# Layer 0 attention of a gated two-layer block: keys and values made once, relu on ScalarE, another TensorE order, and wide magic sums in the last ffn

## The reference

```
# layer 0 attention, x normalised first: 16 heads of 16 channels, scale = 16 ** -0.5
q = x_norm @ Wq + bq;  k = ctx @ Wk + bk;  v = ctx @ Wv + bv
attn = softmax(clip(q @ k.T * scale, -10000, 10000), axis=-1)
x = x + tanh(g) * ((attn @ v) @ Wo + bo)
...
# layer 1 ffn, hidden of 1024 channels in 8-bit weights and 16-bit activations
h = gelu(x_q @ W_in_q + b_in)
h_q = clip(round(h * s), -32768, 32767) / s,  s = 32767 / max(abs(h))
x = x + tanh(g) * (h_q @ W_out_q + b_out)
```

## Time and profile before

| | us |
|---|---|
| median of 3 runs | 1312.31 |
| the profiled execution, its own time | 1310.7 |
| its span | 1308.6 |
| attention of layer 0, from its first load to the last output tile | 7.0 to 325.1 |
| last block of the ffn, from its first magic sum | 1234.2 to the end |
| TensorE busy | 1180.4 (90%) |
| VectorE busy | 977.9 (75%) |
| ScalarE busy | 812.1 (62%) |
| GpSimd busy | 540.7 (41%) |

### The profile page before, as it was taken

How to read it: one execution, slowest core, us unless ns; L and a number is a source line. 1 busy time by engine, 2 the same in 40 slices (tenths; PEclk the granted TensorE clock), 3 DMA queues, 4 the chain that set the end, 5 groups by cost and what they waited for, 6 DMA issues and landing times. The chain is left out here.

```text
span 1308.6 us, 26405 instructions
## 1 busy us (share of the span) xinstructions
PE 1180.4 (90%) x8487; PEld 895.5 (68%) x8533; DVE 977.9 (75%) x2135; ACT 812.1 (62%) x2405; POOL 540.7 (41%) x523
## 2 busy tenths in 40 slices
PE   4989999897786599999999999975999999959898
PEld 3879888886443377777777777753777777735465
DVE  4988989895763356666666667745999999869798
ACT  2454646453466356666666665535888888739897
POOL 3666757674313322222222222106888889600000
PEclk9999999999799699999999999997999999979899
DMA  3223323221976425333333333215424242100133
GB/s 120 66 73 97 97 72 99 72 85 37 281 226 198 129 55 153 116 114 118 115 116 115 116 116 101 78 46 149 139 74 143 74 143 74 62 8 1 33 105 122
DMA packets 124157, 135.30 MB, mean 103 GB/s; under 512 B 13837, under 2 KB 108739, under 8 KB 123907
## 3 DMA queue, kind: packets, MB, share of 16 engines
q1 hardware_dynamic: 116577, 114.81, 28.2%
q0 software_dynamic: 6816, 18.62, 5.2%
q10 hardware_dynamic: 642, 0.33, 0.1%
HBM read 84.43 MB, written 49.29 MB: 102 GB/s over the span
## 5 line engine op out<-in xcount | busy, mean ns | idle before, releaser
L1424 ACT ACTIVATE exp_h<-exp_ps_h,exp_b_now 128x256 f32<-128x256 f32 x312 | 128.7, 463 | 159.8 <-PE exp_ps_h L1364 156.5
L1338 POOL DMA_INDIRECT exp_xg<-xn,all_token_of x78 | 94.5, 1212 | 311.6 <-PE exp_ps_x L1351 291.9
L1364 PE MATMUL exp_ps_h<-exp_xhi,exp_w_now 128*128 128x256 bf16 x1248 | 214.8, 276 | 4.5 <-DVE exp_xlo L1455 4.5
L1809 ACT ACTIVATE a_z<-a_ps_sc,a_nmx 128x77 f32<-128x77 f32 x512 | 159.2, 367 | 36.0 <-DVE a_nmx L1911 36.0
L1364 PE MATMUL exp_ps_h<-exp_xlo,exp_w_now 128*128 128x256 bf16 x624 | 172.1, 276 | 0.0
L1531 DVE TENSOR_TENSOR exp_hlo<-exp_h,exp_hhi 128x512 bf16<-128x512 f32 x156 | 106.9, 692 | 79.5 <-ACT exp_hhi L1428 76.9
L1376 PE MATMUL exp_ps_y<-moe_w2s,exp_hhi 128*128 x585 | 139.2, 379 | 2.0
L1364 PEld LDWEIGHTS exp_ps_h<-exp_xhi,exp_w_now 128*128 128x128 bf16 x1248 | 123.5, 99 | 20.6 <-issue 5.1
L1809 ACT ACTIVATION_READ_ACCUMULATOR a_z<-a_ps_sc,a_nmx 128x1 f32 x512 | 127.8, 250 | 0.0
L1776 PE MATMUL a_ps_o<-a_v_now,a_phi 128*128 128x256 bf16 (+1 forms) x640 | 106.6, 273 | 2.3 <-DVE a_plo L1900 2.3
L1428 ACT ACTIVATE exp_hhi<-exp_h 128x512 bf16<-128x512 f32 x156 | 98.3, 630 | 4.9
(11 more groups left out here) (243 smaller groups left out, 2858.8 us busy)
## 6 DMA issues: line engine op xcount, KB each, us to landing
a_stage<-in_L_ffn_W_dram SPq DMA_DIRECT2D x64, 256.0 KB
y_slots<-exp_y SPq DMA_DIRECT2D x78, 128.0 KB
fold_k<-route_kst SPq DMA_DIRECT2D x16, 308.0 KB, 4.2
fold_v<-route_vst SPq DMA_DIRECT2D x16, 308.0 KB
exp_job_in<-fold_k SPq DMA_DIRECT2D x14, 352.0 KB
exp_job_in<-fold_v SPq DMA_DIRECT2D x14, 352.0 KB
a_x<-in_x_dram SPq DMA_DIRECT2D x32, 128.0 KB, 2.5
x<-a_xo SPq DMA_DIRECT2D x32, 128.0 KB, 1.7
```

What stands on the lines that cost most here:

```text
L1338: pool.indirect_dma_start(out=xg[:, v, u, :], out_offset=None, in_=xn_dram[:, :], in_offset=bass.IndirectOffsetOnAxis(ap=at.bitcast(U32), ...
L1364: mm = pe.matmul(ps_h[:, i, f % 2 * SLOT_T:(f % 2 + 1) * SLOT_T], w1_now[:, v, k, hl, f * P:(f + 1) * P], xx[:, k, :], start=(q == 0), sto ...
L1424: ins = act.activation(h[:, f, :], ps_h[:, i, f % 2 * SLOT_T:(f % 2 + 1) * SLOT_T], ACT.Gelu_apprx_tanh, bias=b1_now[:, v, f:f + 1])
L1809: ins = act.activation(z[:, u, h * KEYS:(h + 1) * KEYS], ps_sc[:, j, (h - SB[j][0]) * KEYS:(h - SB[j][0] + 1) * KEYS], ACT.Exp, bias=nmx[: ...
```

## The change

In `attention` the keys and values of all four batches are multiplied once, near the start: keys of batch 0 before the loop, values in slot 0 (two pairs of batches, 8 matmuls of 256 columns), the keys of batches 1 to 3 in slot 1. ScalarE copies them to `kT` and `v_rows`. The block diagonals now have two buffers each; GpSimd sets them to zero once (four memsets instead of masks), and SyncE puts the keys and values of each batch in their places by transfers inside SBUF: 8 for the keys (slot t = 6 of the batch before) and 25 for the values (slots t = 2 to 5 of the batch before, four heads in each; for batch 0 all 25 in slot 1). TensorE waits for `k_in` at t = 0 and for `v_in` at t = 2. The functions `block_keys`, `block_values` and `context` are gone.

`min(z, 0)` on VectorE becomes `relu(-z)` on ScalarE, followed there by exp with the sign turned. z has three buffers. On TensorE the output projection comes right behind the queries, and the transposes of the probabilities go behind the scores. ScalarE copies the queries before relu and exp; VectorE takes the sums of exp behind the maxima; GpSimd adds the bias and makes one low half before the products with the reciprocals. All slots are written out, without a loop. `wq` and `bq` are loaded by ScalarE's queue on a semaphore of their own.

In the last block of `ffn` the magic sums are wide: VectorE does blocks 0 and 1 in one instruction of 1024 columns, ScalarE blocks 2 to 4 and 5 to 7 in two of 1536 columns. The group loop is written out.

```diff
+            def place_keys(b):
+                sp.wait_ge(s["kT_done"], 1 if b == 0 else 2)
+                wait(sp, s["scores_done"], NSB * TPB * (b - 1))
+                for h in range(hpg):
+                    rows = slice(h * dh, (h + 1) * dh)
+                    sp.dma_start(kblk[rows, b % 2, :, h * KEYS:(h + 1) * KEYS], kT[rows, :, b, :]).then_inc(k_in[b % 2], 16)
+            def place_values(b, h0, h1):
+                sp.wait_ge(s["v_rows_done"], b // 2 + 1)
+                wait(sp, s["pv_done"], TPB * (b - 1))
+                for h, r0, r1 in spans:
+                    if h0 <= h < h1:
+                        i = blocks.index((r0 // P, h // hpg))
+                        sp.dma_start(vblk[r0 % P:r0 % P + r1 - r0, b % 2, i, h % hpg * dh:(h % hpg + 1) * dh],
+                                     v_rows[r0 - h * KEYS:r1 - h * KEYS, b, h * dh:(h + 1) * dh]).then_inc(v_in[b % 2], 16)
...
# SyncE, end of a slot
+                if T == 1:
+                    sp.wait_ge(s["zero_done"], 4)
+                    place_values(0, 0, HEADS)
+                if t == 6 and b + 1 < B:
+                    place_keys(b + 1)
+                if 2 <= t < 6 and b + 1 < B:
+                    place_values(b + 1, 4 * (t - 2), 4 * (t - 2) + 4)
...
# TensorE
-                if has(T - 2):
-                    pe.wait_ge(s["norm_done"], T - 1)
-                    if t == 2:
-                        pe.wait_ge(s["v_done"], NVG * (b + 1))
...
                 if has(T - 3):
                     pe.wait_ge(s["attn_done"], T - 2)
...
+                if has(T - 2):
+                    pe.wait_ge(s["norm_done"], T - 1)
+                    if T == 2:
+                        pe.wait_ge(s["kT_done"], 2)
...
...
+                if T == 0:
+                    pe.wait_ge(weights_in, 16 * N_WEIGHTS)
+                    values(0, 2)
+                    values(1, 1)
+                if T == 1:
+                    pe.wait_ge(s["v_rows_done"], 2)
+                    keys(1, B, 0)
...
# ScalarE, behind attnT and qT
+                if has(T - 1):
+                    zt = z[:, (T - 1) % NZ, :]
+                    act.wait_ge(s["z_done"], NSB * T)
+                    act.activation(zt, zt, ACT.Relu, scale=-1.0).then_inc(s["zc_done"], 1)
+                    act.wait_ge(s["zc_done"], T)
+                    act.activation(zt, zt, ACT.Exp, scale=-scale).then_inc(s["exp_done"], 1)
...
# VectorE
-                    dve.wait_ge(s["z_done"], NSB * (T + 1))
-                    dve.tensor_scalar(z[:, u, :], z[:, u, :], 0.0, None, ALU.min).then_inc(s["zc_done"], 1)
...
# last block of ffn, ScalarE
+            DVE_F = 2
+            ACT_PARTS = ((DVE_F, 5), (5, FCH))
...
                     for f in range(FCH):
-                        if f + 1 < FCH:
-                            scale(g, f + 1)
-                        elif has(g + 1):
-                            scale(g + 1, 0)
-                        high(g, v, f)
+                        if g == 0 and f == 2:
+                            scale(0, 1)
+                        high(g, v, f)
+                        if has(g + 1) and f == 2:
+                            scale(g + 1, 0)
+                        if has(g + 1) and f == 5:
+                            scale(g + 1, 1)
```

More of the change, by code:

```diff
@@ L165, in attention @@
     pieces = pieces_of(hpg)
-    vgroups = [blocks[i:i + 4] for i in range(0, len(blocks), 4)]
-    NVG = len(vgroups)
-    RING, SKEW = 8, 3
+    spans = []
+    for h in range(HEADS):
+        lo, hi = h * KEYS, (h + 1) * KEYS
+        cuts = [lo] + [c * P for c in range(RCH + 1) if lo < c * P < hi] + [hi]
+        spans += [(h, r0, r1) for r0, r1 in zip(cuts, cuts[1:])]
+    RING, SKEW, NZ = 8, 3, 3
     with ExitStack() as ctx:
@@ L205, in attention @@
         keys_in, weights_in, gbo_done = m.sem("keys_in"), m.sem("weights_in"), m.sem("gbo_done")
+        queries_in = m.sem("queries_in")
+        k_in = [m.sem(f"k_in{i}") for i in range(2)]
+        v_in = [m.sem(f"v_in{i}") for i in range(2)]
         x_loaded = [m.sem(f"x_loaded{i}") for i in range(RING)]
@@ L280, in power @@
                 pool.tensor_tensor(rstd[:, u:u + 1], veps[:, u:u + 1], C.half[:, 0:1], ALU.pow).then_inc(s["rstd_done"], 1)
[L283 to L290, removed]
+            pool.memset(kblk[:, 0, :, :], 0.0).then_inc(s["zero_done"], 1)
             power(0, 0)
             power(1, 1)
[L293 to L302, removed]
+            pool.memset(vblk[:, 0, :, :], 0.0).then_inc(s["zero_done"], 1)
+            pool.memset(kblk[:, 1, :, :], 0.0).then_inc(s["zero_done"], 1)
+            pool.memset(vblk[:, 1, :, :], 0.0).then_inc(s["zero_done"], 1)
             pool.wait_ge(weights_in, 16 * N_WEIGHTS)
@@ L421, in slot @@
                             n = min(P, ROWS - c * P)
-                            mm = pe.matmul(ps_v[:, g * P:(g + 1) * P], vblk[0:n, i, :], pT[0:n, c, :],
+                            mm = pe.matmul(ps_v[:, g * P:(g + 1) * P], vblk[0:n, bv % 2, i, :], pT[0:n, c, :],
                                            start=(i == mine[0]), stop=(i == mine[-1]))
                     mm.then_inc(s["pv_done"], 1)
-                if has(T) and t == 1:
-                    wait(pe, s["pT_done"], 3 * (T - 1))
-                    values()
-                if has(T + 1) and t == TPB - 1:
-                    keys(T + 1, b + 1)
+                if T == 0:
[5 more added lines that the diff above has]
+                    keys(1, B, 0)
             run(pe, slot)
@@ L567, in slot @@
                     ln_mean(T + 2, u)
-                if has(T - 2) and t == 2:
-                    if isinstance(T, int) and T == 2:
-                        dve.wait_ge(s["mask_step"], MASKS)
-                    block_values(T - 2, b)
-                if has(T - 1):
-                    sums(T - 1, (t - 1) % 2)
                 if has(T - SKEW):
@@ L589, in slot @@
                                           ALU.max).then_inc(s["max_done"], 1)
+                if has(T - 1):
+                    sums(T - 1, (t - 1) % 2)
+                if has(T):
                     dve.wait_ge(s["max_done"], NSB * (T + 1))
```

243 lines of the change are left out of this document (102 added, 141 removed).

## The result

The changed kernel takes 1293.68 us (median of 4 runs, 1293.07 to 1294.22) against 1312.84 for the kernel before, run beside it (4 runs, 1310.56 to 1313.88): a ratio of 0.985 [0.983, 0.987]. It is faster, as forecast, but by 19 us where 38 were forecast, and just above the range. The profiled execution took 1293.61, with a span of 1291.8: 16.8 less than before, where the sum said 37.8. So 21.0 us have to be found.

The account below looks back on a forecast made before the run. TensorE's work plus a 0.54 us wait of the scores for copied queries was taken to bound the attention slot, with batch turns extra. Terms -9.8 - 22.2 - 0.8 - 3.0 - 2.0 = -37.8 gave 1274 us, range 1263 to 1293.

Parts of the forecast that it names:

- A slot in the middle: Attention's middle slots: the scores' wait shrinks, a slot falls from 8.24 to 7.89 us; -9.8 us over 28 slots.
- The turns: Three batch turns in attention: their extra 7.4 us each vanishes if transfers are in time; -22.2 us.
- SyncE's queue: Attention slots with new transfers: issues of 0.33 to 0.43 us leave weight pieces hidden by 0.7 to 1.2 us.
- The start: First attention slots: earlier scores and later value placement nearly cancel; -0.8 us, bounds -4 and +3.
- rival 2: Attention: transfers become the new wait, by issues of 0.85 us or late landing; 1300 us, chance 0.10.
- The end: Attention from queries of slot 31 to last output: 21.9 us instead of 24.9; -3.0 us (0 to -5).
- The ffn: Last ffn block: wide magic sums bring groups from 8.43 to 8.0 us; -2.0 us (-0.5 to -3.5).
- 1, the clip: Attention: VectorE's clip of the maxima waits 2.25 us for GpSimd over SBUF; 1305 us, chance 0.07.
- 3, the gap stays: Attention: relu dearer than exp, or pT behind it, keeps the slot at 8.24 us; 1284 us, chance 0.12.
- 4, table loads: Attention: relu and exp need different ScalarE tables, two 1.283 us loads a slot; 1343 us, chance 0.03.

Follow-up runs that it names:

- e7: Changed kernel with min(z, 0) back on VectorE and exp alone on ScalarE, the rest as changed: 1294.86 us (one run).
- e5: Changed kernel with TensorE's transposes of the probabilities put back behind the queries, ahead of output projection and scores: 1318.89 us (one run).
- e6: Changed kernel with relu and exp put back ahead of the copy of the queries on ScalarE: 1338.27 us (one run).
- e1: Changed kernel with the key and value transfers of batches 1 to 3 spread over all eight slots: 1286.79 us, 0.9804 of the kernel before.
- e4: Changed kernel without 22 of batch 0's 25 value transfers and without all value transfers of batches 1 to 3: 1271.78 us (one run).
- e3: Changed kernel, later transfers spread over eight slots, first value products earlier, 11 of batch 0's 25 value transfers issued by ScalarE: 1273.87 us, 0.9707 of the kernel before.
- e11: Changed kernel, values placed by way of DRAM, first value products earlier, later transfers spread over eight slots, SyncE alone issuing: 1270.41 us, 0.9668 of the kernel before.
- e9: Changed kernel plus 54 probe transfers on SyncE behind the attention, varying source, partitions and row size: 1338.77 us (one run).
- e10: Changed kernel with copied values stored to DRAM and the same 25 value transfers a batch read from there: 1280.53 us (one run).

## Why the prediction was half right

*A slot in the middle*: right. 7.89 forecast, 7.92 measured. Two reasons in it were wrong. The min did not have to leave VectorE: e7 shows that its move brings 2 us at most of the some 9, and none in an undisturbed slot. The prediction's own sum left VectorE 0.2 + 0.45 + 1.3 us free in the new slot, enough for it. And the transposes had to move for GpSimd's products, not for the scores: without their new place a slot is 8.81 (e5), without that of the query copy 9.68 (e6). Each of the two is needed, but how the 9 us divide is not shown, since no run puts one of the new orders, or the third buffer of z, into the kernel before by itself.

*The turns*: right. The wait of 2.97 and the value products of 4.63 have no successor, and in e1 all 28 slots are alike.

*SyncE's queue*: this step failed. It priced an issue too low and so had the weight pieces hidden by 0.7 to 1.2 us; they came up to 1.32 us late in eight slots, and 12.19 late in slot 2. "An issue takes 0.33 to 0.43" was taken from L256, loads from DRAM. The new transfers lie inside SBUF. All issues of the changed kernel's two new lines:
```profile
L257 SPq DMA_DIRECT2D a_vblk<-moe_w1s x100: 555/758/1200, 27.5 to 211.8; - x100
L248 SPq DMA_DIRECT2D a_kblk<-a_kT x32: 586/593/1240, 14.3 to 222.3; - x32
```
I gave the weight pieces a margin of 0.7 to 1.2 us behind eight issues of 0.4, so it is gone at some 0.5 to 0.6 an issue; eight of 0.59 take 4.7 us, seven of 0.76 take 5.3. It is rival 2's mechanism, with the price I had allowed it (0.85) nearly met, but with eight late slots where it had 15 (its own terms, 15 x 1.2 + 10, give 1302, not 1300). I gave it 0.10 on the ground that 0.85 had been seen once, though no row of the kernel before showed a transfer inside SBUF, and the bounds should have been carried to the end. The Trainium skill (DMA: Bandwidth & Descriptors, Issuing engines are not separate DMA queues) says that spreading DMAs over several issuing engines only saves issue time, usually small against the DMA; this case does not bear out "usually small": an issue inside SBUF takes 0.59 or 0.76 where a key transfer lands 1.9 after its issue, and issue time was the cost. The value transfers cost 19.8 us (e4), and e3 is 19.8 faster than the changed kernel by starting earlier, spreading and sharing.

*The start*: -0.8 forecast, +9.8 measured, the same failed price (19.70 instead of about 10) and a consequence that I had left out: TensorE stood idle for 12.74 and went on at half its clock, 2.4 us more for the first value products and 0.7 in the next slot. The keys felt it too: their eight issues took 5.21, and TensorE waited 3.88 for them, so the scores of tile 0 began at 20.83, forecast 20.4. Two other terms were too high: the value products took 3.63, not 5, at a granted clock of 1.00, and the queries of tile 2 came at 34.15, not 36.4. In e11 the queries of slot 3 come at 42.55, 4.7 before the 47.29 of the kernel before. (Output tile 0 is 7.2 earlier there, but 2.5 of that is its earlier place in the slot.)

*The end*: right. 21.9 forecast and measured.

*The ffn*: -2.0 forecast, -1.7. By form in the last block:
```profile
L2156 ACT ACTIVATE ffn_hid<-ffn_hid,f_magic,ffn_h_scale 128x1536 f32<-128x1536 f32 x16 | 26.5, 1653 | 4.0 <-DVE f_magic L2208 4.0
L2190 DVE TENSOR_SCALAR ffn_hid<-ffn_hid,ffn_h_scale 128x1024 f32<-128x1024 f32 x8 | 6.0, 749 | 0.0
```
The sum of 1536 columns takes 1.65 (1.56 from start to start) against 1.54, the one of 1024 0.75 against 0.71.

*The rivals.* 1, the clip: it did go first, with a median of 0.11 and 0.97 at the most:
```profile
L580 DVE TENSOR_SCALAR a_mx<-a_mx x32: 109/110/970, 25.4 to 292.3; 128x16 f32<-128x16 f32 x32
```
The long ones are those that begin while GpSimd makes a low half of the weights, and they end with it:
```profile
144.89 1.15 POOL L331 TENSOR_TENSOR moe_w1s<-a_stage,moe_w1s 128x512 bf16<-128x512 f32 x1 [2.75 <-ACT moe_w1s L486]
145.29 0.79 DVE L580 TENSOR_SCALAR a_mx<-a_mx 128x16 f32<-128x16 f32 x1
```
With the Trainium skill's rule that the first to start keeps the shared ports (SBUF — State Buffer, SBUF: two separate sides) this agrees: the clip ends at 146.08, GpSimd's instruction at 146.04. 3, the gap stays: no. 4, table loads: one load in the stage.

What stays open: the 0.15 us for 77 partitions inside SBUF, 2.0 us in stages that the change leaves alone, which lie within the scatter of ten other profiles, and how the gain of the middle slot divides between its parts.

## What to carry to other kernels

When work is turned into transfers, price their issues by a row of the same kind (inside SBUF or from DRAM); if there is no such row, carry the dearest as a full case, and count how many stand in front of the next load that somebody waits for. Spread them until no slot holds more than that load's margin allows. And undo each edit alone before you give it the credit: here the order of TensorE mattered for another wait than the one that it seemed made for, and the move of the min hardly mattered.

## What the runs showed of the hardware

- An issue on SyncE costs 0.58 to 0.60 us when both ends lie in SBUF, and 0.35 to 0.43 from DRAM; with 77 partitions inside SBUF it is 0.75. Inside SBUF neither rows of 64 or 512 bytes nor 1 or 128 partitions change it (e9). On ScalarE's queue the value placements cost 0.78, on SyncE's 0.75 (medians, e3). With the source in DRAM the same value placements are issued in 0.30 each (median, e10), in the changed kernel in 0.76.
- After 12.74 us of idle TensorE the granted clock was 0.50 (1.2 GHz), and products that take 2.69 took 5.04 (changed kernel).
- The 256 KB weight pieces land 3.2 us (median) after their issue, with or without the small transfers inside SBUF before them (changed kernel, e4, e10).
- VectorE's clip of the maxima takes 0.11 alone, and 0.79 when it begins during a GpSimd instruction, with which it ends (changed kernel).
- On ScalarE relu and exp of 1232 columns take the same 1.23 us each, under one table load (changed kernel).
